# Two graph layers on one core: two row vectors are laid over the partitions through memory instead of by sixteen transposes, and the first unit of the score matrix is made later

## The chip, the cores and the metric

The kernel runs on one core of one Trainium2 chip. The metric is the device time of one execution in microseconds (us); lower is better.

## The reference, cut to what matters

Eight batches of a 1024 x 256 input `x` go through two graph layers. Layer 0 normalises `x`, builds a dense 1024 x 1024 matrix T from two score vectors and applies it twice. Layer 1 normalises again, adds the identity to the adjacency, scales it by row sums, and multiplies.

```python
def layer0(X, A):                       # X = relu(layernorm(x)), A = adj
    Xw = X @ Wv + bv
    sj, si = Xw @ aw[:d, 0], Xw @ aw[d:, 0]
    e = leaky_relu(sj[:, None, :] + si[:, :, None] + ab[0], 0.2)
    T = A * exp(e); T = T / (T.sum(-1, keepdims=True) + 1e-12)
    H, Xk = 0, X
    for k in range(3):
        H = H + Xk @ Wk[k] + bk[k]
        Xk = einsum('bij,bjd->bid', T, Xk)
    return relu(H)

def layer1(X, A):                       # X = relu(layernorm(x)) of the new x
    Ah = A + eye
    dh = rsqrt(Ah.sum(-1))
    return relu(einsum('bnm,bmf,fc->bnc', dh[:, :, None] * Ah * dh[:, None, :], X, kernel) + bias)
# x = x + layer0(...);  x = x + layer1(...)
```

## The kernel before, in words

Every product keeps single-precision accuracy by splitting both factors in a high and a low part and adding three products (high-high, high-low, low-high). So each tile that TensorE (PE) reads is rounded by ScalarE (ACT, "high") and its rest is taken by VectorE (DVE) or GpSimd (POOL, "low").

A batch b goes through four stages on PE, each written out by hand on each engine, with semaphores between them:

- **U** (`accumulate`, phase 0): eight chunks i of 24 matmuls, T times (X W2). Chunks 1 to 4 are each followed by one `out_product` of batch b-1 (six matmuls). After chunk 4 stands `rows_of_mean(b + 1)` (L1003): eight transposes that each turn one column of means `mv0[:, t, 0]`, broadcast to 128 columns, so that the 1024 means of batch b+1 lie as a row on all 128 partitions, in two banks of PSUM.
- **Dense** (`layer0_dense(b + 1)`, L1063): for eight tiles t six matmuls of 512 columns into `da` and six of 258 into `db`. Between the two of tile t, PE waits on `p0_ready` until DVE has read `db` of tile t-1 (there is one `db` bank), and then makes one transpose `si_rows(t - 1)` (L1015) of a column of scores. The last one, `layer0_end`, stands after the first chunk of V.
- **V** (`accumulate`, phase 1): eight chunks of 24 matmuls, T times the result of U.
- **Z** (`layer1_piece`): sixteen pieces of six matmuls of 512 columns. Piece q needs the rounded half tile `a_ready` and, for q under 8, the tile `hs_ready` of the normalised input.

The work for the next batch lies beside these stages. T of batch b+1 is made in eight units u: ACT adds the scores and applies the leaky function (`leaky`, four instructions on L471) and the exponential (`exponent`, L477), DVE multiplies with the adjacency (`t_prod`, L747), ACT rounds (`t_high`, L485) and DVE takes the rest (`t_low`, L752). The tables `SCORE_V`, `HIGH_V`, `PROD_V`, `LOW_V` say after which chunk of V each unit's step stands; unit 0 is scored inside the dense stage (after tiles 4 and 5) and multiplied there (after tile 6).

Layer norm of batch b+1 needs on DVE: `stats0_of` (L646, two tiles after each of chunks 0 to 3 of U, table `STATS_U`), `moments0` (L637, L641), and `centre` (L686), which takes the row of means off the transposed input `xt`, for its first two groups after chunks 5 and 6 of U. ACT rounds it (`centred_hi`, L403, ahead of chunks 6 and 7), DVE takes the rest (`centred_lo`, L692). The dense stage starts when group 0 of these is ready.

In U, ACT also sums the rows of the adjacency (`rows`, L502), in the order of `ROWS_U`: tile 2 after chunk 2, tiles 5 and 6 after chunk 4, tile 7 after chunk 5. SyncE (SP) issues the loads in one written order: in U it loads row tiles 4 to 7, each when the slot of tile t-4 is free, and after each stores one output tile of batch b-1. `g1_hi` (L524) is ACT's rounding of each chunk of U, `u_chunk` (L765 to L772) DVE's reading of it.

Of the kernel before, what the change touches and what calls it, by code (L numbers as in the profile page):

```python
# [5 lines left out]
F32 = mybir.dt.float32  # L6
# [13 lines left out]
def gnn_two_layers(nc, x, x_t, adj, adj_t, adj_z, wv_t, vecs, wk, bk, w_l1, bias_l1, out):  # L20
# [11 lines left out]
    SCORE_V = {-1: 1, 2: 2, 3: 3, 5: 4}  # L32
    HIGH_V = {1: (0, 1), 5: (2,)}
    PROD_V = {0: 1, 3: 2, 5: 3, 7: 4}
# [11 lines left out]
    STATS_U = {0: (0, 1), 1: (2, 3), 2: (4, 5), 3: (6, 7)}  # L46
# [14 lines left out]
    with ctx:  # L61
# [70 lines left out]
        bv_r = sb("bv_r", [P, KD, P])  # L132
        v_s = sb("v_s", [P, KD + 1, 2])
# [19 lines left out]
        mean_rows = [tp[:, r].rearrange("p k c -> p (k c)") for r in range(2)]  # L153
# [12 lines left out]
        def si_tile(t):  # L166
            return acc[:, SI_SLOT, t % 4 * P:(t % 4 + 1) * P]

# [35 lines left out]
        nb1_ready = sem("nb1_ready")  # L204
        xt_loaded = [sem(f"xt_loaded{g}") for g in range(NG)]
        x_loaded = [sem(f"x_loaded{g}") for g in range(NG)]
        mean_full, xt_centred = sem("mean_full"), sem("xt_centred")
# [40 lines left out]
        def _(sp):  # L248
# [99 lines left out]
        def _(pool):  # L348
# [26 lines left out]
            def batch(b, last):  # L375
                for i in range(NT):
                    g1_split(b, i)
                    if i == (3 if b > 0 else -1) and not last:
# [17 lines left out]
        def _(act):  # L396
            def centred_hi(g, b):
# [48 lines left out]
            def si_copy(b, g):  # L446
                act.wait_ge(si_full, b * NG + g + 1)
                nc.scalar.copy(si[:, g * 2 * P:(g + 1) * 2 * P],
                               acc[:, SI_SLOT, g % 2 * 2 * P:(g % 2 + 1) * 2 * P]).then_inc(si_ready, 1)

            def leaky(b, u):
# [13 lines left out]
                if u % 2 == 0:  # L465

                    act.wait_ge(si_ready, b * NG + u // 2 + 1)
# [22 lines left out]
            def layer0_dense(b, after):  # L490
                for t in range(NT):
# [3 lines left out]
                    if t % 2 == 0 and t > 0:  # L495
                        si_copy(b, t // 2 - 1)
# [19 lines left out]
            def batch(b, par, last):  # L516
                for i in range(NT):
                    if i == 0 and b > 0:
                        zt_high(b - 1, 1)
                    if i >= NT - 2 and not last:  # L520
# [12 lines left out]
                def after(t):  # L533
# [86 lines left out]
        def _(dve):  # L620
# [201 lines left out]
            def batch(b, par, left):  # L822
                last = left == 0
                for i in range(NT):
# [4 lines left out]
                    u_chunk(b, i)  # L829
                    if i in (NT - 3, NT - 2) and not last:  # L830
# [8 lines left out]
                    if not last and b > 0:  # L839
                        for t in STATS_U.get(i, ()):  # L840
                            stats0_of(b + 1, t)
                        if i == 3:
                            moments0(b + 1)
                def after(t):
# [135 lines left out]
        def _(pe):  # L980
# [22 lines left out]
            def rows_of_mean(b):  # L1003
# [5 lines left out]
                for t in range(NT):  # L1009
                    ins = nc.tensor.transpose(mean_rows[t // HJ][:, t % HJ * P:(t % HJ + 1) * P],  # L1010
                                              mv0[:, t, 0:1].to_broadcast([P, P]), ident[:, :])
                    if t % HJ == HJ - 1:
                        ins.then_inc(mean_full, 1)

            def si_rows(b, t):  # L1015

                if t == 0 and b > 0:

                    pe.wait_ge(g1_tmp_ready, b * NT)
                if t % 2 == 0 and t > 0:  # L1020

                    pe.wait_ge(si_ready, b * NG + t // 2)
                ins = nc.tensor.transpose(si_tile(t), sij[:, t, 1:2].to_broadcast([P, P]), ident[:, :])  # L1023
                if t % 2:
                    ins.then_inc(si_full, 1)
# [37 lines left out]
            def layer0_dense(b):  # L1063
# [3 lines left out]
                for g in range(NG):  # L1067
# [3 lines left out]
                    for s in range(2):  # L1071
# [13 lines left out]
            def layer0_end(b):  # L1085
                pe.wait_ge(p0_ready, b * NT + NT)
                si_rows(b, NT - 1)
# [30 lines left out]
            def accumulate(b, phase, i, read, before, ready, n, rhs):  # L1118
# [8 lines left out]
                for jt in range(NT):  # L1127
                    if ready is not None and i == 0:
# [8 lines left out]
            def batch(b, last):  # L1137

                pe.wait_ge(g2_ready, b * NT + NT)
                for i in range(NT):  # L1140
                    if i % 2 == 0:
# [3 lines left out]
                               lambda jt: (g2_hi[:, jt, :], g2_lo[:, jt, :]))  # L1145
                    if i in OUT_U and b > 0:
                        out_product(b - 1, OUT_U[i])
                    if i == HJ and not last:
                        rows_of_mean(b + 1)
# [3 lines left out]
                for i in range(NT):  # L1153
                    if i == 1 and not last:
                        layer0_end(b + 1)
# [93 lines left out]
```

## Time and profile before

| what | value |
| --- | --- |
| median of 3 runs | 773.25 us (772.89 to 774.9) |
| the profiled execution, its own time | 775.14 us |
| its span in the trace | 772.9 us |
| mean granted TensorE clock | 0.998 of full speed |
| DVE, ACT, POOL busy | 79%, 70%, 24% of the span |

The profiled execution is 2.24 us longer than its span and 1.89 us above the median. Times in rows are microseconds from the start of the span. PE is the matmul engine, PEld its weight load; matmuls overlap, so the distance between two starts, not the length of one, is what a matmul takes of PE's time. SPq and ACTq are the DMA issues of SP and ACT.

### The profile page before, as it was taken

The numbers are of one execution on the slowest core, as the hardware profiler recorded it, in microseconds if no ns is written. First come the engines' busy times: TensorE is split into PE (matmuls) and PEld (weight loads), VectorE is DVE, ScalarE is ACT, GpSimd is POOL, SyncE is SP. The second block draws the span as 40 slices with busy tenths as digits, with TensorE's granted clock in tenths as the row PEclk, the third lists the DMA queues.
The fourth block names the chain that finished last, engine by engine and source line by source line (L and its number), as shares of the span: only waits on it lengthen the run. The fifth ranks groups of instructions, "written<-read, shape, count | busy, mean of one in ns | idle before, by whom it ended". The sixth has DMA issues, their size and how long they took to land.

```text
span 772.9 us, 14177 instructions
## 1 busy us (share of the span) xinstructions
PE 758.8 (98%) x5190; PEld 695.6 (90%) x5190; DVE 610.9 (79%) x1420; ACT 539.6 (70%) x1051; POOL 183.9 (24%) x184
## 2 busy tenths in 40 slices
PE   8699999999999999999999999999999999999997
PEld 8498988989899898998989989899998989889986
DVE  6986888778896789967888678886888777895665
ACT  3988797567966679657785578856698567976351
POOL 1031240312403123130321405123050321402330
PEclk9999999999999999999999999999999999999999
DMA  6846339624497055970569505784148733356411
GB/s 226 298 137 193 120 132 320 225 96 137 138 317 263 20 154 177 299 243 1 177 208 302 187 13 184 255 272 150 69 144 303 240 118 109 133 209 210 140 62 54
DMA packets 60660, 135.93 MB, mean 176 GB/s; under 512 B 6320, under 2 KB 32304, under 8 KB 60592
## 3 DMA queue, kind: packets, MB, share of 16 engines
q1 hardware_dynamic: 51824, 104.35, 41.1%
q10 hardware_dynamic: 8768, 30.68, 11.4%
q8 instruction: 41, 0.67, 0.4%
q14 instruction: 27, 0.22, 0.1%
HBM read 126.62 MB, written 8.39 MB: 175 GB/s over the span
## 4 chain that ended last, share of the span: by engine, by line
PE 90%; DVE 4%; ACT 4%; issue 1%; DMA 1%; SPq 0%; DVEq 0%
PE acc L1132 16%; PE acc L1134 16%; PE acc L1133 16%; PE da L992 11%; PE db L992 6%; PE da L1102 4%; PE da L1100 4%; PE da L1101 4%; PE tp L1100 4%; PE tp L1102 4%; PE tp L1101 4%; ACT tg_e L471 2%; PE acc L1023 1%; ACT g_hi L439 1%; PE tp L1010 1%
## 5 line engine op out<-in xcount | busy, mean ns | idle before, releaser
L1132 PE MATMUL acc<-g_hi,t_hi 128*128 128x256 f32 (+1 forms) x1024 | 291.9, 285 | 2.8 <-DVE g_lo L721 2.8
L1134 PE MATMUL acc<-g_hi,t_lo 128*128 128x256 f32 (+1 forms) x1024 | 290.3, 284 | 0.0
L1133 PE MATMUL acc<-g_lo,t_hi 128*128 128x256 f32 x1024 | 289.6, 283 | 0.0
L1132 PEld LDWEIGHTS acc<-g_hi,t_hi 128*128 128x128 f32 x1024 | 194.1, 190 | 3.5 <-issue 3.2
L1133 PEld LDWEIGHTS acc<-g_lo,t_hi 128*128 128x128 f32 x1024 | 194.6, 190 | 0.3
L1134 PEld LDWEIGHTS acc<-g_hi,t_lo 128*128 128x128 f32 x1024 | 194.5, 190 | 0.0
L366 POOL TENSOR_TENSOR g_lo<-tmp,g_hi 128x256 fp32r<-128x256 f32 x64 | 58.6, 916 | 265.8 <-ACT g_hi L524 265.8
L471 ACT ACTIVATE tg_e<-si,sij 128x256 f32<-128x256 f32 x256 | 109.3, 501 | 4.0 <-DVE sij L708 4.0
L758 DVE TENSOR_TENSOR a_lo<-a_raw,a_hi 128x512 fp32r<-128x512 f32 x128 | 89.7, 720 | 25.1 <-ACT a_hi L514 25.1
L361 POOL TENSOR_TENSOR rstd<-ve,mhalf 128x2 f32<-128x2 f32 (+2 forms) x41 | 51.3, 1251 | 193.6 <-DVE ve L658 144.9
L524 ACT CAST g_hi<-tmp 128x256 fp32r<-128x256 f32 x64 | 25.9, 404 | 101.1 <-DVE tmp L772 101.1
L514 ACT CAST a_hi<-a_raw 128x512 fp32r<-128x512 f32 x128 | 76.9, 619 | 18.5 <-DVE a_raw L797 11.6
L372 POOL TENSOR_TENSOR hs_lo<-tmp,hs_hi 128x256 fp32r<-128x256 f32 x64 | 60.2, 960 | 81.0 <-ACT hs_hi L416 81.0
L477 ACT ACTIVATE tg_e<-tg_e 128x1024 f32<-128x1024 f32 x64 | 67.9, 1061 | 1.2
L747 DVE TENSOR_TENSOR t_raw<-tg_a,tg_e 128x1024 f32<-128x1024 f32 x50 | 60.9, 1219 | 9.7 <-ACT tg_e L477 9.7
L502 ACT ACTIVATE a_raw<-a_raw 128x1024 f32<-128x1024 f32 x64 | 67.3, 1053 | 0.0
L752 DVE TENSOR_TENSOR t_lo<-t_raw,t_hi 128x1024 fp32r<-128x1024 f32 x50 | 62.0, 1240 | 0.0
L412 ACT ACTIVATE tmp<-p,nb,rstd 128x256 f32<-128x256 f32 x64 | 34.9, 593 | 38.1 <-DVE nb L662 37.9
L485 ACT CAST t_hi<-t_raw 128x1024 fp32r<-128x1024 f32 x50 | 52.2, 1043 | 0.4 <-DVE t_raw L747 0.4
L765 DVE TENSOR_SCALAR row_t<-acc 128x1 f32<-128x1 f32 x64 | 9.9, 155 | 52.7 <-PE acc L1134 52.7
L726 DVE SCALAR_TENSOR_TENSOR g_lo<-da,rstd,g_hi 128x256 fp32r<-128x256 f32 x56 | 27.1, 484 | 30.1 <-ACT g_hi L439 30.1
L1100 PE MATMUL tp<-a_hi,hs_hi 128*128 128x512 f32 x128 | 50.8, 397 | 0.0
(146 smaller groups left out, 1635.0 us busy)
## 6 DMA issues: line engine op xcount, KB each, us to landing
a_raw<-adj_dram SPq DMA_DIRECT2D x64, 512.0 KB, 4.6
a_raw<-adj_z_dram SPq DMA_DIRECT2D x64, 512.0 KB, 3.9
tg_a<-adj_t_dram ACTq DMA_DIRECT2D x58, 512.0 KB, 4.4
x_o<-x_dram SPq DMA_DIRECT2D x64, 128.0 KB, 2.5
out_dram<-x_o SPq DMA_DIRECT2D x64, 128.0 KB, 3.5
x_nat<-x_dram SPq DMA_DIRECT2D x28, 256.0 KB, 4.3
xt<-x_t_dram SPq DMA_DIRECT2D x28, 256.0 KB, 4.5
tg_a<-adj_t_dram SPq DMA_DIRECT2D x6, 512.0 KB, 4.0
```

The costliest lines, as they stand in the source:

```text
L471: ins = nc.scalar.activation(tg_e[:, s, :, q, :], si[:, c].rearrange("p (s i) -> p s i", s=2), ACT.Prelu, bias=sij[:, jt, 0:1], alpha=SLOPE)
L477: nc.scalar.activation(tg_e[:, u % TS], tg_e[:, u % TS], ACT.Exp).then_inc(e_ready, 1)
L502: nc.scalar.activation(a_raw[:, t % RS, :], a_raw[:, t % RS, :], ACT.Copy, accum_out=row_a[:, t:t + 1]).then_inc(rows_done, 1)
L514: nc.scalar.copy(a_half(a_hi, i, h), a_raw[:, i % RS, h * N // 2:(h + 1) * N // 2]).then_inc(a_hi_done[h], 1)
L752: nc.vector.tensor_tensor(t_view(t_lo, u), t_parts(b, u), t_view(t_hi, u).bitcast(F32), ALU.subtract).then_inc(t_ready, 1)
L758: nc.vector.tensor_tensor(a_half(a_lo, i, h), a_raw[:, i % RS, h * N // 2:(h + 1) * N // 2], a_half(a_hi, i, h).bitcast(F32), ALU.subtract ...
L992: ins = nc.tensor.matmul(dst[:, 0:n], l, r, start=(c == 0 and a == 0), stop=(c == len(pairs) - 1 and a == 2))
L1100: nc.tensor.matmul(zt[r][:, f, :], l_hi, r_hi, start=(jt == 0), stop=False)
L1101: nc.tensor.matmul(zt[r][:, f, :], l_hi, r_lo, start=False, stop=False)
L1132: nc.tensor.matmul(acc[:, s, 0:n], l_hi, r_hi, start=(jt == 0), stop=False)
L1133: nc.tensor.matmul(acc[:, s, 0:D], l_hi, r_lo, start=False, stop=False)
L1134: ins = nc.tensor.matmul(acc[:, s, 0:n], l_lo, r_hi, start=False, stop=(jt == NT - 1))
```

## The change

The means of batch b+1 are turned with one transpose of `mv0[:, :, 0]` (128 x 8) into an 8 x 128 corner of PSUM. ACT copies it into SBUF (`mean_t`), SP stores it to a 4 KB tensor in memory (`mean_rows_dram`), waits until it has landed, and reads it back with one DMA that writes all 1024 means on each of the 128 partitions, into the buffer `si`, whose scores of batch b are no longer needed. `centre` takes the means from there. The transpose stands in the middle of chunk 3 of U (chunk 1 for the first batch). The statistics move to chunks 0 and 1 of U (four tiles each), and `rstd0` on POOL to chunk 1.

The scores go the same way in two halves of four tiles: one transpose ahead of `db` of tile 4 of the dense stage and one in the middle of chunk 0 of V, a copy of 4 x 128 by ACT, a store of 2 KB, and a read of 512 scores to all partitions.

The first unit of T is scored and multiplied after tile 7 of the dense stage; unit 1 moves in V from before chunk 0 to after it (scores) and from chunk 0 to 1 (product), its rounding from chunk 1 to 2.

```diff
-    SCORE_V = {-1: 1, 2: 2, 3: 3, 5: 4}
-    HIGH_V = {1: (0, 1), 5: (2,)}
-    PROD_V = {0: 1, 3: 2, 5: 3, 7: 4}
+    SCORE_V = {0: 1, 2: 2, 3: 3, 5: 4}
+    HIGH_V = {1: (0,), 2: (1,), 5: (2,)}
+    PROD_V = {1: 1, 3: 2, 5: 3, 7: 4}
-    STATS_U = {0: (0, 1), 1: (2, 3), 2: (4, 5), 3: (6, 7)}
+    STATS_U = {0: (0, 1, 2, 3), 1: (4, 5, 6, 7)}
 # SP
+            def mean_over_partitions(b):
+                sp.wait_ge(mean_t_ready, b)
+                sp.dma_start(mean_dram, mean_t).then_inc(mean_stored, 16)
+                sp.wait_ge(mean_stored, 16 * b)
+                sp.wait_ge(leaky_done, b * NU)
+                sp.dma_start(si[:, :], mean_dram.rearrange("t (o p) -> o (t p)", o=1).to_broadcast([P, N])).then_inc(mean_loaded, 16)
+            def si_over_partitions(b, h):
+                sp.wait_ge(si_t_ready, 2 * (b - 1) + h + 1)
+                sp.dma_start(si_dram[h], si_t).then_inc(si_stored, 16)
+                sp.wait_ge(si_stored, 16 * (2 * (b - 1) + h + 1))
+                sp.wait_ge(xt_centred, (b - 1) * NG + 2 * h + 2)
+                sp.dma_start(si[:, h * HJ * P:(h + 1) * HJ * P],
+                             si_dram[h].rearrange("(o t) p -> o (t p)", o=1).to_broadcast([P, HJ * P])).then_inc(si_loaded[h], 16)
             def batch(b, left):
                 for i in range(HJ):
                     rows(b, (RS + i,))
                     if b > 0:
                         stores(b - 1, HJ + i)
+                    if i == 1 and left > 0 and b > 0:
+                        mean_over_partitions(b + 1)
...
                 for i in range(NT):
+                    if i == 2 and left > 0:
+                        si_over_partitions(b + 1, 0)
+                        si_over_partitions(b + 1, 1)
 # ACT
+            def mean_copy(b):
+                act.wait_ge(mean_full, b)
+                nc.scalar.copy(mean_t, mean_bank).then_inc(mean_t_ready, 1)
+            def si_copy(b, h):
+                act.wait_ge(si_t_full, 2 * (b - 1) + h + 1)
+                if h == 1:
+                    act.wait_ge(si_stored, 16 * (2 * b - 1))
+                nc.scalar.copy(si_t, si_bank).then_inc(si_t_ready, 1)
                 for i in range(NT):
+                    if i == (1 if b == 0 else 3) and not last:
+                        mean_copy(b + 1)
...
-                    if t == 4 and not last:
-                        leaky(b + 1, 0)
-                    if t == 5 and not last:
-                        exponent(b + 1, 0)
                     if t == 7:
                         a_round(b, 1, 1)
+                        if not last:
+                            leaky(b + 1, 0)
+                            exponent(b + 1, 0)
 # DVE
-                dve.wait_ge(mean_full, 2 * (b - 1) + g // 2 + 1)
-                row = mean_rows[g // 2][:, g % 2 * 2 * P:(g % 2 + 1) * 2 * P]
+                dve.wait_ge(mean_loaded, 16 * b)
+                row = si[:, g * 2 * P:(g + 1) * 2 * P]
-                    if t == 6 and not last:
-                        t_prod(b + 1, 0)
                     if t == 7:
                         a_low(b, 1, 0)
                         a_low(b, 1, 1)
+                        if not last:
+                            t_prod(b + 1, 0)
 # PE
-                for t in range(NT):
-                    ins = nc.tensor.transpose(mean_rows[t // HJ][:, t % HJ * P:(t % HJ + 1) * P],
-                                              mv0[:, t, 0:1].to_broadcast([P, P]), ident[:, :])
+                nc.tensor.transpose(mean_bank, mv0[:, :, 0], ident[:, :]).then_inc(mean_full, 1)
+            def si_turned(b, h):
+                if h == 0:
+                    pe.wait_ge(g1_tmp_ready, b * NT)
+                else:
+                    pe.wait_ge(si_t_ready, 2 * b - 1)
+                pe.wait_ge(p0_ready, b * NT + HJ * (h + 1))
+                nc.tensor.transpose(si_bank, sij[:, h * HJ:(h + 1) * HJ, 1], ident[:, :]).then_inc(si_t_full, 1)
                         pe.wait_ge(p0_ready, b * NT + t)
-                        if t > 0:
-                            si_rows(b, t - 1)
+                        if t == HJ:
+                            si_turned(b, 0)
```

## Rows read from the trace of the kernel before

**Rows 1.** The page: busy time of PE, and the chain that ended last, by engine.

```profile
PE 758.8 (98%) x5190; PEld 695.6 (90%) x5190; DVE 610.9 (79%) x1420; ACT 539.6 (70%) x1051; POOL 183.9 (24%) x184
...
PE 90%; DVE 4%; ACT 4%; issue 1%; DMA 1%; SPq 0%; DVEq 0%
```

**Rows 2.** Groups by line of PE, shapes apart: busy us, mean ns.

```profile
L1023 PE MATMUL acc<-ident,sij 128*128 128x128 f32 x56 | 16.3, 292 | 0.7
...
L1010 PE MATMUL tp<-ident,mv 128*128 128x128 f32 x56 | 7.2, 272 | 0.0
```

**Rows 3.** The chain in order of time: start us, us of the span, what.

```profile
148.84 0.87 PE tp L1010 x8
...
158.32 1.39 PE da L992 x6
159.71 0.72 PE db L992 x6
```

**Rows 4.** The timeline of PE: first matmuls of U, dense, V and Z of batch 1.

```profile
131.44 0.28 PE L1132 MATMUL acc<-g_hi,t_hi 128*128 128x258 f32 x1
...
158.16 0.39 PE L992 MATMUL da<-wa_hi,ht_hi 128*128 128x512 f32 x1
...
176.40 0.28 PE L1132 MATMUL acc<-g_hi,t_hi 128*128 128x256 f32 x1
...
199.51 0.39 PE L1100 MATMUL da<-a_hi,hs_hi 128*128 128x512 f32 x1
```

**Rows 5.** Who waited for whom: us in total, times, longest.

```profile
PEld acc L1023 <- DVE sij L708: 10.1, 29, 0.5
```

**Rows 6.** The timeline of ACT and DVE in the dense stage: [idle before <- releaser].

```profile
169.51 0.37 ACT L448 COPY si<-acc 128x256 f32<-128x256 f32 x1
169.76 1.72 ACT L471 ACTIVATE tg_e<-si,sij 128x256 f32<-128x256 f32 x4
...
172.08 1.07 ACT L477 ACTIVATE tg_e<-tg_e 128x1024 f32<-128x1024 f32 x1
...
172.24 0.48 DVE L726 SCALAR_TENSOR_TENSOR g_lo<-da,rstd,g_hi 128x256 fp32r<-128x256 f32 x1 [0.58 <-ACT g_hi L439]
```

**Rows 7.** The timeline of ACT and DVE in U of batch 1.

```profile
136.77 0.74 DVE L646 BATCH_NORM_STATS2 st<-x_nat 128x6 f32<-128x256 f32 x2
...
142.45 1.06 ACT L502 ACTIVATE a_raw<-a_raw 128x1024 f32<-128x1024 f32 x1
...
147.11 0.65 DVE L637 BATCH_NORM_AGGREGATE mv<-st 128x2 f32<-128x6 f32 x8
...
153.84 1.06 ACT L502 ACTIVATE a_raw<-a_raw 128x1024 f32<-128x1024 f32 x1
...
154.89 0.61 ACT L403 ACTIVATE ht_hi<-xt 128x512 fp32r<-128x512 f32 x1
...
156.88 0.69 DVE L692 SCALAR_TENSOR_TENSOR ht_lo<-xt,ht_hi 128x512 fp32r<-128x512 f32 x1
```

**Rows 8.** DMA issues in windows at 146, 147, 151 and 162 to 181: KB, us to landing.

```profile
out_dram<-x_o SPq DMA_DIRECT2D x1, 128.0 KB, 2.1
...
a_raw<-adj_dram SPq DMA_DIRECT2D x1, 512.0 KB, 3.4
...
a_raw<-adj_z_dram SPq DMA_DIRECT2D x3, 512.0 KB, 4.8
...
x_o<-x_dram SPq DMA_DIRECT2D x1, 128.0 KB, 2.0
```

**Rows 9.** The timeline of ACT and DVE in V and at the start of Z.

```profile
177.68 1.71 ACT L471 ACTIVATE tg_e<-si,sij 128x256 f32<-128x256 f32 x4 [0.56 <-DVE sij L708]
...
191.36 1.22 DVE L747 TENSOR_TENSOR t_raw<-tg_a,tg_e 128x1024 f32<-128x1024 f32 x1 [1.05 <-ACT tg_e L477]
...
203.37 0.68 DVE L758 TENSOR_TENSOR a_lo<-a_raw,a_hi 128x512 fp32r<-128x512 f32 x1
...
206.49 2.44 DVE L758 TENSOR_TENSOR a_lo<-a_raw,a_hi 128x512 fp32r<-128x512 f32 x3 [0.55 <-ACT a_hi L514]
```

More of the change, by code:

```diff
@@ L132, in gnn_two_layers @@
         bv_r = sb("bv_r", [P, KD, P])
+        mean_t, si_t = bv_r[0:NT, 0, :], bv_r[0:HJ, 1, :]
         v_s = sb("v_s", [P, KD + 1, 2])
@@ L152, in gnn_two_layers @@
         zt = [da, tp.rearrange("p g k c -> p g (k c)")]
-        mean_rows = [tp[:, r].rearrange("p k c -> p (k c)") for r in range(2)]
+        mean_bank = tp[0:NT, 0, 0, 0:P]
+        si_dram = nc.dram_tensor("si_rows_dram", (2, HJ, P), F32, kind="Internal").ap()
+        mean_dram = nc.dram_tensor("mean_rows_dram", (NT, P), F32, kind="Internal").ap()
         ht_first = [g1.rearrange("p t d -> p (t d)").rearrange("p (g k c) -> p g k c", g=NG, k=KD) for g1 in (g1_hi, g1_lo)]
@@ L204, in gnn_two_layers @@
         nb1_ready = sem("nb1_ready")
+        si_t_full, si_t_ready, si_stored = sem("si_t_full"), sem("si_t_ready"), sem("si_stored")
+        si_loaded = [sem(f"si_loaded{h}") for h in range(2)]
         xt_loaded = [sem(f"xt_loaded{g}") for g in range(NG)]
         x_loaded = [sem(f"x_loaded{g}") for g in range(NG)]
-        mean_full, xt_centred = sem("mean_full"), sem("xt_centred")
+        mean_full, mean_t_ready, mean_stored, mean_loaded, xt_centred = (
+            sem(n) for n in ("mean_full", "mean_t_ready", "mean_stored", "mean_loaded", "xt_centred"))
         hs_hi_done, hs_ready = sem("hs_hi_done"), sem("hs_ready")
@@ L336, in _ @@
                         load_xt(1, g)
+            mean_over_partitions(1)
             for b in range(0, B - 3, 2):
@@ L377, in batch @@
                     g1_split(b, i)
-                    if i == (3 if b > 0 else -1) and not last:
+                    if i == (1 if b > 0 else -1) and not last:
                         power(rstd0, ve0, ve0_ready, b + 1, rstd0_ready)
@@ L464, in leaky @@
                     act.wait_ge(p0_ready, b * NT + (u + 1) * HJ)
-                if u % 2 == 0:
-                    act.wait_ge(si_ready, b * NG + u // 2 + 1)
+                if b == 0 and u % 2 == 0:
+                    act.wait_ge(si_ready, u // 2 + 1)
+                elif b > 0 and u % HJ == 0:
+                    act.wait_ge(si_loaded[u // HJ], 16 * b)
                 c = slice(u // 2 * 2 * P, (u // 2 + 1) * 2 * P)
@@ L494, in layer0_dense @@
                     dense0(b, t)
-                    if t % 2 == 0 and t > 0:
-                        si_copy(b, t // 2 - 1)
+                    if t == HJ:
+                        si_copy(b, 0)
                     after(t)
@@ L829, in batch @@
                     u_chunk(b, i)
+                    if not last and b > 0:
+                        for t in STATS_U.get(i, ()):
+                            stats0_of(b + 1, t)
+                        if i == 1:
+                            moments0(b + 1)
                     if i in (NT - 3, NT - 2) and not last:
@@ L838, in batch @@
                         t_low(b, low[i])
[L839 to L843, printed above, removed]
                 def after(t):
@@ L1116, in out_product, with accumulate @@
                                                     for f in range(KD)]).then_inc(out_full, 1)
-            def accumulate(b, phase, i, read, before, ready, n, rhs):
+            def accumulate(b, phase, i, read, before, ready, n, rhs, middle=None):
                 s = acc_slot(phase, i)
@@ L1127, in accumulate @@
                 for jt in range(NT):
+                    if jt == HJ and middle is not None:
+                        middle()
                     if ready is not None and i == 0:
@@ L1144, in batch @@
                     accumulate(b, U_PHASE, i, g1_tmp_ready, v_tmp_done, None, D + 2,
-                               lambda jt: (g2_hi[:, jt, :], g2_lo[:, jt, :]))
+                               lambda jt: (g2_hi[:, jt, :], g2_lo[:, jt, :]),
+                               middle=(lambda: rows_of_mean(b + 1)) if i == (1 if b == 0 else 3) and not last else None)
                     if i in OUT_U and b > 0:
                         out_product(b - 1, OUT_U[i])
-                    if i == HJ and not last:
-                        rows_of_mean(b + 1)
                 if not last:
@@ L1153, in batch @@
                 for i in range(NT):
-                    if i == 1 and not last:
-                        layer0_end(b + 1)
                     if i == 2 and not last:
-                        pe.wait_ge(si_ready, (b + 2) * NG)
+                        pe.wait_ge(si_t_ready, 2 * (b + 1))
                     accumulate(b, V_PHASE, i, v_tmp_done, g1_tmp_ready, g1_ready, D,
-                               lambda jt: (g1_hi[:, jt, :], g1_lo[:, jt, :]))
+                               lambda jt: (g1_hi[:, jt, :], g1_lo[:, jt, :]),
+                               middle=(lambda: si_turned(b + 1, 1)) if i == 0 and not last else None)
                 dense = b + 1 if last else b + 2
```

22 lines of the change are left out of this document (3 added, 19 removed).

## The prediction, made before the changed kernel was run

> **What bounds it now.** I read the page first, then the chain in order of time, the waits of PE, and the timeline of batch 1 with its four stages. PE is busy 758.8 of 772.9 us and holds 90% of the chain that ended last [rows 1]; the reader is to see that almost every matmul taken away is time taken away. Outside the first 40 us and the last 2 us PE has no waits but one kind: before the score transposes it waits for DVE's `sij`, 29 times, 10.1 us in total on the weight-load side [rows 5]. Much of that 10.1 us is the previous matmul still streaming, so it isn't the price; the stage's length is. The starts of the stages of batch 1 give U 26.72 us, dense 18.24, V 23.11, Z from 199.51 on [rows 4]. A tile of the dense stage needs 1.39 + 0.72 = 2.11 us of issue [rows 3], eight of them 16.9, so the dense stage holds 18.24 - 16.9 = 1.35 us of transposes and stalls.
>
> **What PE loses.** There are seven transitions to a next batch.
>
> Means: eight transposes take 0.87 us in the chain [rows 3], 0.11 each, though each lasts 272 ns [rows 2]. One remains: 0.76 us saved per transition, all of it on PE's path. I take for the new form (8 columns in, 8 x 128 out) the same 0.11; bounds 0.05 to 0.27 (its full length), a hundredth or so of the sum. The Trainium skill, "TensorE: Matmul & The Clock Gate", Part 4 on the PE-mode transpose, gives about 275 ns for one in a kernel's context. Its length agrees with the 272 ns of the trace, but thirteen removed per transition at 275 ns would be 25 us, and the distances in the chain say 0.11 each; the distances decide.
>
> Scores: of the seven in the dense stage one remains, and the one after chunk 0 of V remains inside it. Without waits that is 6 x 0.11 = 0.66 us. But `p0_ready` stays: PE waits there for DVE with or without a transpose. I went through the tiles on ACT and DVE. Around tile 3 DVE runs without a pause (a diagonal, `centred_lo`, `centre`, then the tile), so `db` of tile 3 starts where the transpose started, 8.1 us into the stage, and the 0.22 saved before becomes a stall of about 0.35. Behind it the stage runs freely, because the second stall goes: now ACT puts 1.71 us of `leaky` and an exponential of 1.06 us among tiles 4 and 5, after which DVE waits 0.58 us for ACT's `g_hi` and PE for DVE [rows 6]. Both move behind tile 7, and ACT also loses three copies of 0.37 [rows 6] here and gains one. New length: 16.9 + 0.11 + 0.35 = 17.4, so 0.85 saved per transition. The least is nothing at all (DVE as the pace, below), the most 1.24 (no stall).
>
> **What the mean's way through memory costs.** The cover is the rest of U, and the queues behind it are what matters. DVE now does eight statistics (0.37 each, the pair 0.74 with its overlap) and the aggregates (0.65 and the add) before chunk 2 where it did four [rows 7]: chunk 2 is read 2.1 us later, at 143.9 by the clock of this batch instead of 142.0. PE needs it only for chunk 5, at 149. ACT's rounding of chunk 2 and row sum 2, now at 142.45 [rows 7], end at 145.4, and `mean_copy` follows, 0.25 to 0.37 by the copy in [rows 6]: 145.7. The transpose at 143.1 is ahead of it. SP then stores 4 KB: the quiet store in [rows 8] takes 2.1 us for 128 KB, so 147.8. The read of 512 KB on all partitions: 3.4 us for one row tile alone, 4.8 for three in a row [rows 8], so 151.3 to 152.6, where `centre` stands at 152.7. Nearly free.
>
> SP waits while it does this, and row tiles 6 and 7 are behind it. Tile 6 is issued at 148.2 (now 143.6) and lands at 148.2 + 4.8 = 153.0 at most; ACT reaches its sum at 150.6 and waits. From its landing R: row sum 6 (1.15 with its read-out), `g1_hi` 0.3, row sum 7 1.15, `centred_hi` 0.6, `centred_lo` 0.7 [rows 7], so R + 3.9 = 156.9. PE is ready for the dense stage at 158.16 - 0.76 = 157.4. Slack 0.5 us; I take no stall, and every us beyond it is a us of stall per transition. In the trace of before the same `centred_lo` ends at 157.6, 0.6 ahead of PE. The Trainium skill, "DMA: Bandwidth & Descriptors", Anatomy of one DMA, puts a DMA at 2.0 us plus its bytes at 436 GB/s; an estimate from that page is 2.0 for the store and 3.2 for each 512 KB, which would leave the chain some 1.5 us more room than the rows do. It also says that the wait is "surprisingly long" above all for a write to HBM, which is the store here.
>
> The scores' first half: transposed 10.2 us into the stage, copied by 11.5, stored and read back by 2.1 + 2.0 to 3.4 [rows 8], at 15.6 to 17.0; memory traffic is idle there. Its reader, `leaky(0)`, stands at 18.0. Free. The second half is needed only for unit 4. SP's load of the residual tile for chunk 2 of V is behind both, 2 us later than now and still ahead of DVE.
>
> **What the later unit 0 costs.** After tile 7 ACT has `leaky` and `exponent` of unit 0 (2.7 us) and then of unit 1 (2.7) where it had only unit 1 [rows 9]. DVE waits for the first (`t_prod(0)` at 3.4 us into V), so chunk 0 is read 1.7 us later, which PE doesn't see (it needs it for chunk 3). `t_prod(1)`, 1.2 us, stands at chunk 1 ahead of both `t_low`; chunk 3 of V is read about 0.9 us later, and the product of unit 2, which waits for ACT already [rows 9], some 1.0 later in V. From there DVE had no pause of note until the first `a_lo` of Z at 203.37 to 204.05 [rows 9]. PE needs that for piece 4, at 199.51 + 4 x 1.39 = 205.1: slack 1.0. The next, at 206.49 to 207.2 [rows 9], is needed for piece 6 at 207.9: slack 0.7. So 1.0 later costs about 0.3 us of stall per transition. Bounds: 0 (the shift soaked up) to 1.0 (shift of 1.7, as at chunk 0).
>
> **Sum.** 0.76 + 0.85 - 0.3 = 1.3 us per transition, seven of them 9.2 us. The profiled execution's span of 772.9 would be 763.7, its own 775.14 some 765.9. The median lies 1.89 below the latter: 773.25 - 9.2 = 764.0 us. About 0.3% (2.3 us) is what a measurement here can tell from no change.
>
> **Rivals.**
> 1. The dense stage keeps its length, because `p0_ready` and not the transposes is its pace: the change doesn't do there what it says. For: DVE has no pause around tile 3. Against: before tiles 4 to 7 DVE waits for ACT and ACT for PE. Left are 0.76 x 7 = 5.3, without the stall in Z since V is no nearer: 768.
> 2. SP's queue: row tile 6 late by 0.5 to 1.5 beyond the slack. For: the slack is only 0.5 us and the chain goes through three landings, which vary from 2.0 to 4.8. Against: each was taken near its upper row. Cost 1 us per transition: 771; at 0.5 it is 767.5.
> 3. The tail of V shifts by the whole 1.7 us, the stall in Z is 1.0: 0.6 left per transition, 769.
> 4. The other side: the same queue, but memory is slow to confirm the store or to serve 128 reads of one 4 KB row. It decides once row tile 6 lands more than 0.5 + 1.3 + 0.33 = 2.1 us later than worked out, after 155.1; 2.5 us later in each transition costs 0.4 x 7 over the kernel before: 776. No row shows a read of one row by all partitions alone.
> 5. Neither stall comes and the dense stage reaches 17.0: 0.76 + 1.24 = 2.0, so 759.5.
>
> **Chances.** Forecast with its small deviations (762 to 766.5) 0.5; rival 1 0.1; 2 0.16; 3 0.08; 4 0.06; 5 0.1. Faster by over 0.3% (below 770.9): the forecast, 1, 3, 5 and half of 2, 0.85; within 0.3% 0.09, mostly of 2; slower 0.06. The range takes in the good part of 5 and of 2: 760.5 to 769.5.
>
> **What would show it.** PE's instructions fall by 13 x 7 = 91. The dense stage should be 17.4 long with its one pause at tile 3; U 25.95; `ht_lo` before the dense stage without a PE wait; ACT idle about 2.5 us for a row tile (L502) around chunk 4 of U, with a DMA as its releaser; in Z a pause of PE of some 0.3 at piece 6, released by `a_lo` L758. I am wrong if the first PE wait of a transition is at the start of the dense stage, if the dense stage stays above 18, or if Z grows by more than 0.5 us.

## The result, and the profile after

The changed kernel takes 777.45 us (median of 6 runs, 775.59 to 779.72), the kernel before 773.11 (6 runs): ratio 1.0049, 95% interval 1.003 to 1.0068. The forecast was 764.0, between 760.5 and 769.5. It is slower, and its runs spread over 4 us. The profiled execution of the kernel before is 1.9 us above its median, so the spans below differ by 2.6 us where the medians differ by 4.3.

The page of the changed kernel, as in [rows 1]:

```profile
PE 754.7 (97%) x5099; PEld 682.4 (88%) x5099; DVE 611.7 (79%) x1420; ACT 534.3 (69%) x1044; POOL 185.3 (24%) x184
...
PE 45%; DVE 25%; ACT 17%; issue 7%; DMA 3%; POOL 3%; SPq 0%; ACTq 0%; DVEq 0%; POOLq 0%
```

PE lost its 91 instructions and 4 us of busy time, the span grew from 772.9 to 775.5. The chain tells more: PE held 90% of it, now 45%, and DVE and ACT have 42%. PE now waits for them in every batch.

Where, the stage lengths say. They are distances between first matmuls of stages in the timeline, as in [rows 4]; the table gives means over batches 1 to 6 (U, V, Z of batch b, dense of batch b+1).

| kernel | U | dense | V | Z | time, us |
| --- | --- | --- | --- | --- | --- |
| before | 26.72 | 18.25 | 23.00 | 25.24 | 773.11 |
| forecast | 25.95 | 17.4 | 23.0 | 25.5 | 764.0 |
| changed | 26.82 (26.04 to 27.63) | 17.77 | 22.98 | 26.26 | 777.45 |

U is 26.04, 26.09, 26.11 in three transitions, near the forecast, and 27.47, 27.60, 27.63 in the other three. Z is 1.0 longer in all. The dense stage is 0.48 shorter, 0.37 less than forecast. The long Z and the long U take back everything that PE had gained.

**Ahead of the dense stage.** The timeline of PE, ACT and DVE of the changed kernel, batch 1:

```profile
156.25 0.28 PE L1167 MATMUL acc<-g_hi,t_lo 128*128 128x258 f32 x1
158.04 0.47 PE L1033 MATMUL da<-wa_hi,ht_hi 128*128 128x512 f32 x1 [1.50 <-DVE ht_lo L733]
...
152.69 1.06 ACT L542 ACTIVATE a_raw<-a_raw 128x1024 f32<-128x1024 f32 x1 [3.08 <-DMA a_raw<-adj_dram]
...
155.50 1.06 ACT L542 ACTIVATE a_raw<-a_raw 128x1024 f32<-128x1024 f32 x1 [1.36 <-DMA a_raw<-adj_dram]
...
156.56 0.61 ACT L438 ACTIVATE ht_hi<-xt 128x512 fp32r<-128x512 f32 x1
...
157.20 0.69 DVE L733 SCALAR_TENSOR_TENSOR ht_lo<-xt,ht_hi 128x512 fp32r<-128x512 f32 x1 [1.70 <-ACT ht_hi L438]
```

PE is through with U at 156.4 and stands until 158.04, because `ht_lo`, which DVE starts at 157.20, ends at 157.89. That waited for ACT's rounding at 156.56, which stands in ACT's order behind the sum of row tile 7 at 155.50, and that waited for its load. The issues of SP in the same stretch:

```profile
145.30 0.29 SPq L300 DMA_DIRECT2D mean_rows_dram<-bv_r  x1
146.54 0.33 SPq L304 DMA_DIRECT2D si<-mean_rows_dram  x1
146.92 0.44 SPq L268 DMA_DIRECT2D a_raw<-adj_dram  x1
147.40 0.43 SPq L273 DMA_DIRECT2D out_dram<-x_o  x1
147.88 0.44 SPq L268 DMA_DIRECT2D a_raw<-adj_dram  x1
```

and the landings, from narrow windows at 146.5 (the read of the means), 146.9 (row tile 6) and 147.9 (row tile 7):

```profile
si<-mean_rows_dram SPq DMA_DIRECT2D x1, 512.0 KB, 4.8
...
a_raw<-adj_dram SPq DMA_DIRECT2D x1, 512.0 KB, 5.8
...
a_raw<-adj_dram SPq DMA_DIRECT2D x1, 512.0 KB, 7.6
```

Batch 1 of the changed kernel starts U 1.03 us earlier than that of the kernel before (131.44 in [rows 4]), because the batch ahead of it is shorter:

```profile
130.41 0.28 PE L1165 MATMUL acc<-g_hi,t_hi 128*128 128x258 f32 x1
```

The forecast's instants are by the clock of the kernel before. So both are counted here from the start of U, in us:

| step of batch 1 | forecast | measured |
| --- | --- | --- |
| store of the means issued | 14.3 | 14.9 |
| read of the means issued | 16.4 | 16.1 |
| row tile 6 issued | 16.8 | 16.5 |
| row tile 6 landed | 21.6 at most | 22.3 |
| row tile 7 there for its sum | 23.0 | 25.1 |
| `ht_lo` ends | 25.5 | 27.5 |
| PE ready for the dense stage | 26.0 | 26.0 |

The store began 0.6 late and was faster than taken (1.24 us from its issue to the next one, not 2.1), so row tile 6 was issued 0.3 early. But it took 5.8 us and not 4.8, and landed 0.7 behind the forecast's latest; that alone uses up the slack of 0.5. Row tile 7 took 7.6 us. The forecast names no landing for it; its sum has the row sum of tile 7 start 1.45 behind the landing of tile 6, which is 23.0, and ACT waited 1.36 us for the tile.

The other transitions split by this one load. Row tile 6 lands at 21.8 to 22.0 in all of them. Row tile 7 takes 6.1 to 6.4 us in the three with a short U, where ACT doesn't wait for it, and 7.6 to 7.9 us in the three with a long one. What decides between the two values no run shows.

**In Z.** The timeline of PE of batch 1, changed kernel: pieces 4 and 6, and the first output product.

```profile
204.15 0.39 PE L1133 MATMUL da<-a_hi,hs_lo 128*128 128x512 f32 x1
204.71 0.50 PE L1131 MATMUL da<-a_hi,hs_hi 128*128 128x512 f32 x1 [0.17 <-DVE a_lo L799]
...
207.38 0.40 PE L1133 MATMUL da<-a_hi,hs_lo 128*128 128x512 f32 x1
207.83 0.50 PE L1131 MATMUL da<-a_hi,hs_hi 128*128 128x512 f32 x1
...
216.10 0.40 PE L1133 MATMUL tp<-a_hi,hs_lo 128*128 128x512 f32 x1
216.49 0.39 PE L1033 MATMUL db<-wl_hi,zt_hi 128*128 128x256 f32 x1
```

Starts here are 0.23 apart; before these three they are 0.56, 0.45 and 0.39, so 0.33, 0.22 and 0.16 too long. Behind each pause the first matmul is itself followed 0.10 us late. Together 1.0. The first two pauses are for `a_lo`, the third for `zt_lo` (L845), DVE's part of the first output product. The backlog that makes them, on DVE, rows to be held against 191.36 and 203.37 in [rows 9]:

```profile
191.95 1.23 DVE L788 TENSOR_TENSOR t_raw<-tg_a,tg_e 128x1024 f32<-128x1024 f32 x1 [1.07 <-ACT tg_e L517]
...
203.97 0.68 DVE L799 TENSOR_TENSOR a_lo<-a_raw,a_hi 128x512 fp32r<-128x512 f32 x1
```

V starts at 175.80 instead of 176.40 and Z at 198.78 instead of 199.51. So the product of unit 2 is 16.15 into V (before 14.96), 1.2 later, and the first `a_lo` of Z ends 5.87 into it (before 4.54), 1.3 later, where piece 4 needs it at 5.60.

From there on everything that DVE makes in Z stands 1.33 later than before, counted from the start of Z, down to `zt_lo`. First the kernel before, with the product that reads it, then the changed kernel:

```profile
216.29 0.28 PE L992 MATMUL db<-wl_hi,zt_hi 128*128 128x256 f32 x1
...
214.56 1.28 DVE L804 TENSOR_TENSOR zt_lo<-da,zt_hi 128x512 fp32r<-128x512 f32 x2
```

```profile
215.16 1.28 DVE L845 TENSOR_TENSOR zt_lo<-da,zt_hi 128x512 fp32r<-128x512 f32 x2
```

`zt_lo` ended 16.33 into Z and the product began at 16.78, 0.45 later; now it ends at 17.66 and the product begins at 17.71, 0.05 later. So only 0.40 us of a shift are free there, less than at piece 4 (1.0) or piece 6 (0.7), and the prediction did not price this place. PE stands 0.93 late at that product, the shift less 0.40, and 0.1 for the last restart makes the 1.02 by which Z grew. The pauses ahead of it are instalments of the same 0.93.

### The profile page after: what moved, and what is told of

Its sections match the earlier page's. It is cut to its first block, busy times and chain, and to the rows that moved or that the text cites. A ratio compares the mean times of both kernels' runs of the same rounds, so it can differ in the third digit from the quotient of the medians.

```text
span 775.5 us, 14030 instructions
## 1 busy us (share of the span) xinstructions
PE 754.7 (97%) x5099; PEld 682.4 (88%) x5099; DVE 611.7 (79%) x1420; ACT 534.3 (69%) x1044; POOL 185.3 (24%) x184
## 4 chain that ended last, share of the span: by engine, by line
PE 45%; DVE 25%; ACT 17%; issue 7%; DMA 3%; POOL 3%; SPq 0%; ACTq 0%; DVEq 0%; POOLq 0%
PE da L1033 10%; PE acc L1165 6%; PE acc L1167 6%; PE acc L1166 6%; PE db L1033 5%; ACT tg_e L511 5%; ACT tg_e L517 3%; DVE t_lo L793 3%; DMA a_raw<-adj_dram 3%; ACT tmp L447 3%; DVE t_raw L788 3%; PE tp L1131 2%; PE tp L1133 2%; PE tp L1132 2%; POOL hs_lo L402 2%
## 5 line engine op out<-in xcount | busy, mean ns | idle before, releaser
L542 ACT ACTIVATE a_raw<-a_raw 128x1024 f32<-128x1024 f32 x64 | 67.5, 1055 | 21.8 <-DMA a_raw<-adj_dram 21.6
L473 ACT ACTIVATE p<-da,rstd 128x256 f32<-128x256 f32 x56 | 26.6, 475 | 48.4 <-PE da L1033 48.2
L1131 PE MATMUL da<-a_hi,hs_hi 128*128 128x512 f32 x128 | 52.0, 407 | 1.6 <-DVE a_lo L799 1.0
```

The source lines that it names most:

```text
L1131: nc.tensor.matmul(zt[r][:, f, :], l_hi, r_hi, start=(jt == 0), stop=False)
```

## The experiments

Stage lengths of all of them, made as above, ahead of their single accounts:

| kernel | U | dense | V | Z | time, us | ratio to before (interval) |
| --- | --- | --- | --- | --- | --- | --- |
| a1 mean only | 26.80 (26.36 to 27.44) | 18.35 | 22.96 | 25.23 | 775.07 | 1.0011 (1.0001 to 1.0022) |
| a2 scores, unit 0 | 26.72 | 17.69 | 23.05 | 26.22 | 778.12 | 1.0055 (1.004 to 1.007) |
| a3 unit 0 only | 26.72 | 17.96 | 23.00 | 26.20 | 778.99 | 1.0067 (1.0052 to 1.0082) |
| a4 row tile 6 first | 26.96 (26.11 to 28.1) | 18.04 | 23.01 | 26.25 | 780.62 | 1.0087 (1.0072 to 1.0102) |
| b1 low 2 in Z | 26.38 (25.96 to 27.65) | 17.75 | 22.97 | 26.57 | 778.15 | 1.0055 (1.0035 to 1.0075) |
| b2 row sums later | 25.97 | 17.70 | 23.03 | 26.20 | 772.67 | 0.9978 (0.9968 to 0.9988) |
| b3 both | 25.97 | 17.71 | 23.00 | 26.46 | 774.38 | 1.0003 (0.9994 to 1.0012) |
| b4 mean, row sums later | 25.97 | 18.26 | 23.03 | 25.24 | 769.79 | 0.9944 (0.9929 to 0.9959) |
| c1 leaky ahead | 25.96 | 17.68 | 23.57 | 25.24 | 771.33 | 0.9957 (0.9944 to 0.997) |
| c2 distinct rows | 25.96 | 17.70 | 22.99 | 26.23 | 772.96 | 0.9988 (0.9975 to 1.0) |
| c3 ACT's queue | 25.97 | 17.68 | 22.96 | 26.27 | 772.58 | 0.9979 (0.997 to 0.9988) |
| d1 transpose later | 25.97 | 17.68 | 23.02 | 26.29 | 773.68 | 0.9994 (0.9985 to 1.0003) |

### a1, a2, a3: the change in parts

a1 puts on the kernel before the statistics, `rows_of_mean`, `mean_copy` and `mean_over_partitions` of the change, with one wait more, so that the old score copies don't overwrite means still to be read:

```diff
                 act.wait_ge(si_full, b * NG + g + 1)
+                act.wait_ge(xt_centred, (b - 1) * NG + g + 1)
```

> The kernel before with the means alone laid out through memory (statistics early, one transpose, SP's store and read back); scores and unit 0 as before. Theory 1 (two separate costs: the later unit 0 makes the pauses in Z, SP's round trip makes the pause ahead of the dense stage): Z stays at 25.24, dense at 18.2, U is 26.05 where row tile 7 lands in time and up to 27.6 where not; 768.5 to 773 us. Theory 2 (the 512 KB read of one 4 KB row slows all memory traffic and with it the whole next stages): Z or V grow here too, and the time is above 773.

a2 is the complement: `si_turned`, `si_over_partitions`, the new `si_copy` and the order of units 0 and 1, means as before. a3 takes of that the order alone:

```diff
-    SCORE_V = {-1: 1, 2: 2, 3: 3, 5: 4}
+    SCORE_V = {0: 1, 2: 2, 3: 3, 5: 4}
...
-                    if t == 4 and not last:
-                        leaky(b + 1, 0)
-                    if t == 5 and not last:
-                        exponent(b + 1, 0)
...
                         a_round(b, 1, 1)
+                        if not last:
+                            leaky(b + 1, 0)
+                            exponent(b + 1, 0)
```

> The kernel before with the scores through memory and the later unit 0; means by eight transposes as before. Theory 1: U stays 26.72 with no pause ahead of the dense stage, dense falls to 17.8, V by 0.1, Z grows to 26.25; net +0.4 per transition, 775.5 to 776.5 us. Theory 2: Z stays near 25.3 and the time falls to about 770.

> The kernel before with nothing but the order of units 0 and 1 changed (scores by transposes as before). Theory 1: Z grows to 26.2, dense loses its second stall (18.25 to about 17.95); net +0.7 per transition, about 778 us. Rival: Z's pauses come from the residual tiles or chunk loads that SP issues later behind its waits for the scores; then Z stays 25.24 and the time is 771 to 773.

The stages fall apart cleanly. The long Z belongs to a2 and a3 and not to a1; in a3 no score goes through memory, no SP issue has moved, and Z is 26.20. So the later unit 0 alone makes the pauses in Z, and the way of the scores through memory doesn't. The uneven U belongs to a1 alone. a1 came out 2 us above the range given for it, but not as theory 2 has it: Z and V did not grow, and its U is above 26.3 in all six batches of its profile. a2 and a3 were 1 to 2 us above theirs, with stages within 0.15 of those expected. Of each of these misses 0.9 us is the kernel before, which took 774.1 us beside these runs. a3 against a2 also prices the scores' way: without their transposes the dense stage is 0.27 shorter (17.96 to 17.69).

### a4: row tile 6 ahead of the mean, a miss

```diff
                     rows(b, (RS + i,))
+                    if i == 2 and left > 0 and b > 0:
+                        mean_over_partitions(b + 1)
                     if b > 0:
                         stores(b - 1, HJ + i)
-                    if i == 1 and left > 0 and b > 0:
-                        mean_over_partitions(b + 1)
```

> The changed kernel with row tile 6 issued ahead of SP's wait for the mean (the store and read back follow it). If the place in SP's order is what delays ACT: ACT no longer waits for row tile 6, the dense stage starts without a pause, U is 26.0 in every transition, 771 to 772 us. If the slow read itself is the cause (row tile 7 still behind it lands after 7 us): U stays between 26.1 and 27.5 and the time between 773 and 777.

Neither case: ACT no longer waits for row tile 6, but it is the slowest kernel of all. SP's issues of a4, batch 1:

```profile
145.88 0.33 SPq L268 DMA_DIRECT2D a_raw<-adj_dram  x1
146.25 0.33 SPq L300 DMA_DIRECT2D mean_rows_dram<-bv_r  x1
149.30 0.34 SPq L304 DMA_DIRECT2D si<-mean_rows_dram  x1
```

The same 4 KB store that took 1.24 us when the last load was issued 3.2 us ahead of it takes 3.05 us when a 512 KB load is issued 0.37 us ahead of it (2.9 to 3.3 in all six transitions). Counted from the start of U, the read of the means goes 2.0 us later and row tile 7 1.5 us later, and now `centre` waits for the means too:

```profile
153.74 0.69 DVE L727 TENSOR_TENSOR xt<-xt,si 128x512 f32<-128x512 f32 x1 [1.30 <-DMA si<-mean_rows_dram]
...
155.35 1.06 ACT L542 ACTIVATE a_raw<-a_raw 128x1024 f32<-128x1024 f32 x1 [2.47 <-DMA a_raw<-adj_dram]
```

ACT waits for tile 7 alone, and that is enough: U is 26.10 to 28.10. One dense stage of this profile, from 628.04 on, was 19.33 long. There PE's granted clock was 0.50, its lower level of 1.2 GHz, after PE had stood idle for 1.98 us, the longest pause ahead of a dense stage in this profile (columns: length, PE, PEld, DVE, ACT, POOL busy, clock, DMA share, GB/s):

```profile
629.00:631.50 2.50, 2.50 (x11) 2.21 (x10) 1.09 (x3) 1.20 (x4) 1.27 (x1) 0.50 0.46 166
```

The stage lost 1.5 us by it in this execution.

### b2, b4: ACT's order

```diff
-    ROWS_U = {0: (0,), 1: (1,), 2: (2,), 3: (3, 4), 4: (5, 6), 5: (7,)}
+    ROWS_U = {0: (0,), 1: (1,), 2: (2,), 3: (3, 4), 4: (5,), 5: (6,), 6: (7,)}
```

b2 is this line on the changed kernel, b4 on a1.

> The changed kernel with ScalarE's sums of row tiles 6 and 7 one chunk later, so that row tile 7 is no longer ahead of the rounding of the centred input. SP's order and all DMAs stay. If the path is row tile 7's landing, ScalarE's order, start of the dense stage: U is 25.9 to 26.1 in every transition, Z stays 26.25; about 773.5 to 774.5 us with little spread between runs. If instead the read of the means itself lands too late: U keeps its values of up to 27.6.

> The kernel with the means alone through memory, and ScalarE's sums of row tiles 6 and 7 one chunk later. Two separate costs: U 26.0, dense 18.3, V 23.0, Z 25.24, about 0.7 us per transition less than before: 769 us.

No DMA moved, and U is 25.97 in every batch of both. The sum of row tile 7 now stands behind the first rounding of the centred input, and its landing no longer reaches PE. b2's ten runs lie between 772.52 and 772.87; the 4 us of spread are gone with the wait. b4 keeps the old unit 0, has the short U and the short Z, and at 769.79 is the fastest kernel of the study. b2 came out 0.8 us below its range, b4 0.8 above its figure.

### c2, c3: what made row tile 7 late

c2 keeps every issue and wait, but reads 128 different rows of 4 KB in place of the same one 128 times (what is subtracted as the mean in the first layer norm of batches 1 to 7 is then not the mean, so its output is not that of the reference):

```diff
-                sp.dma_start(si[:, :], mean_dram.rearrange("t (o p) -> o (t p)", o=1).to_broadcast([P, N])).then_inc(mean_loaded, 16)
+                sp.dma_start(si[:, :], adj_v[b, :, 0]).then_inc(mean_loaded, 16)
```

> The changed kernel, but the read of the means takes 512 KB from 128 different rows of the adjacency in place of 128 times the same 4 KB row (so the first layer norm subtracts other numbers than the means). All waits, issues and bytes stay. If the repeated row is slow to read: this transfer lands in about 3.5 instead of 4.8 us, row tiles 6 and 7 land 1 us earlier, U is 26.0 in nearly all transitions, 773.5 to 774.5 us. If only the place in the queue counts: landings and time as in the changed kernel, 775.5 to 779.

The transfer lands in 4.2 us (median of seven) instead of 4.6, row tile 6 behind it in batch 1 in 5.0 instead of 5.8, row tile 7 in 5.6 to 5.9 in all six transitions instead of 6.1 to 7.9, and U is 25.96 or 25.97 throughout its profile. The stretch from 149 to 151, first of the changed kernel, then of c2 (PE, PEld, DVE, ACT, POOL busy, clock, DMA share, GB/s):

```profile
149.00:151.00 2.00, 2.00 (x19) 2.00 (x19) 0.16 (x1) 0.62 (x2) 0.58 (x1) 1.00 0.94 244
```

```profile
149.00:151.00 2.00, 2.00 (x19) 2.00 (x18) 0.36 (x1) 1.00 (x2) 0.93 (x1) 1.00 0.91 330
```

With nearly the same share of the DMA engines' time, the kernel with the repeated row moves 244 GB/s and the other 330. At the same place of batch 2 (243.1 to 245.1, and 241.8 to 243.8 in c2) it is 211 GB/s at a share of 0.75 against 337 at 1.00. So a part of row tile 7's delay is the repeated row: in batch 1 it lands in 5.9 us and not 7.6, which is most of what it took beyond 4.8, and ACT waits 0.35 us for it and not 1.36. One of c2's ten runs took 776.22; it was not the profiled one, so whether the wait came back in it is not shown.

c3 has ACT issue the store (chunk 3 of U) and the read (chunk 4) of the means from its own queue:

```diff
                 nc.scalar.copy(mean_t, mean_bank).then_inc(mean_t_ready, 1)
+                act.wait_ge(mean_t_ready, b)
+                act.dma_start(mean_dram, mean_t).then_inc(mean_stored, 16)
```

> The changed kernel with the store of the means and their read issued by ScalarE (the store at chunk 3 of U, the read at chunk 4) instead of SP, so that SP waits for neither. If SP's waits delay the row tiles: row tile 6 is issued 2 us earlier and ScalarE doesn't wait for it, row tile 7 lands by 153, U is 26.0 to 26.1, about 773 us. If the transfers themselves crowd the row tiles out: ScalarE still waits for row tile 7 and U stays up to 27.5.

U is 25.97, and ACT waits for no row tile in batches 1 to 6. The read goes 1.5 us later from the start of U (at 148.44), now behind row tile 7, and takes 5.4 us, so DVE waits for it instead, which PE doesn't notice:

```profile
153.78 0.69 DVE L734 TENSOR_TENSOR xt<-xt,si 128x512 f32<-128x512 f32 x1 [1.68 <-DMA si<-mean_rows_dram]
```

So SP's round trip ahead of the two loads, the repeated row and ACT's order are three conditions of one stall, and taking away any one of them is enough (for the repeated row, in nine of ten runs). Moving the round trip behind row tile 6 alone, as in a4, is not enough.

### b1, b3, c1, d1: the pauses in Z

b1 takes DVE's `t_low` of unit 2 out of V; b3 is b1 with the later row sums.

```diff
-    LOW_V = {1: 0, 2: 1, 6: 2}
+    LOW_V = {1: 0, 2: 1}
-    LOW_Z, LOW_U = {1: 3, 7: 4, 12: 5, 15: 6}, {1: 7}
+    LOW_Z, LOW_U = {1: 2, 3: 3, 7: 4, 12: 5, 15: 6}, {1: 7}
```

> The changed kernel with the low part of unit 2 taken after piece 1 of Z instead of after chunk 6 of V (and that of unit 3 after piece 3), 1.2 us less for VectorE ahead of the first tiles that Z waits for. If VectorE's backlog from the later unit 0 makes the pauses in Z: Z falls from 26.25 to about 25.3, U and dense as in the changed kernel; 777.4 - 6.5 = 771 us. If the pauses have another source (the residual tiles or chunks of the adjacency landing late): Z stays at 26.25.

> Both edits on the changed kernel. Theory of two separate costs: U 26.0, dense 17.8, V 23.0, Z 25.3, that is 1.25 us per transition less than the kernel before: 765 us. If the two costs hide one another, or a third wait stands behind them: above 768 us.

Wrong as a cure. The pause at piece 4 goes, a longer one stands at piece 6, and Z is 0.3 longer than without the edit. (b1 also kept the stall of U, 27.65 in one batch.) b3, batch 1, PE, ACT and DVE:

```profile
207.10 0.50 PE L1131 MATMUL da<-a_hi,hs_hi 128*128 128x512 f32 x1 [0.65 <-DVE a_lo L799]
...
204.10 0.60 ACT L447 ACTIVATE tmp<-p,nb,rstd 128x256 f32<-128x256 f32 x1 [1.55 <-DVE nb L703]
...
203.91 0.16 DVE L703 SCALAR_TENSOR_TENSOR nb<-mv,rstd 128x2 f32<-128x2 f32 x1 [0.59 <-POOL rstd L391]
...
206.35 1.84 DVE L799 TENSOR_TENSOR a_lo<-a_raw,a_hi 128x512 fp32r<-128x512 f32 x2 [0.54 <-ACT a_hi L554]
...
200.26 0.16 DVE L699 SCALAR_TENSOR_TENSOR ve<-mv,row_a 128x2 f32<-128x2 f32 x1
...
200.33 2.43 POOL L402 TENSOR_TENSOR hs_lo<-tmp,hs_hi 128x256 fp32r<-128x256 f32 x2 [1.91 <-ACT hs_hi L451]
202.73 1.14 POOL L391 TENSOR_TENSOR rstd<-ve,mhalf 128x2 f32<-128x2 f32 x1
```

DVE has time now, and waits itself: for ACT's `a_hi`, ACT for `nb`, `nb` for POOL's `rstd`. The input of `rstd`, `ve`, is there at 200.42, but POOL first works off two `hs_lo`, and takes 2.43 us for them (1.60 in the changed kernel). Why these took longer was not tested. Everything behind is then 1.55 late instead of 1.33: taking 1.2 us from one engine only names the next.

That a shift, and not the number of pauses, sets Z can be read from `zt_lo` of batch 1 in five kernels:

| kernel | `zt_lo` ends, us into Z | later than before | less 0.40, plus 0.10 | Z longer than before |
| --- | --- | --- | --- | --- |
| before | 16.33 | | | |
| c1 (below) | 16.50 | 0.17 | none | 0.00 |
| changed | 17.66 | 1.33 | 1.03 | 1.02 |
| d1 (below) | 17.79 | 1.46 | 1.16 | 1.17 |
| b3 | 17.88 | 1.55 | 1.25 | 1.24 |

c1 gets the backlog out where it comes in. With the later row sums of b2, unit 0's leaky function stands ahead of tile 7 of the dense stage (the scores have landed at 174.0 in the changed kernel, 170.86 + 3.1), and unit 1's product and rounding are back in chunks 0 and 1:

```diff
-    HIGH_V = {1: (0,), 2: (1,), 5: (2,)}
-    PROD_V = {1: 1, 3: 2, 5: 3, 7: 4}
+    HIGH_V = {1: (0, 1), 5: (2,)}
+    PROD_V = {0: 1, 3: 2, 5: 3, 7: 4}
...
+                        if not last:
+                            leaky(b + 1, 0)
                     if t == 7:
                         a_round(b, 1, 1)
                         if not last:
-                            leaky(b + 1, 0)
                             exponent(b + 1, 0)
```

> The changed kernel with ScalarE's sums of row tiles 6 and 7 one chunk later (as in b2), and unit 0 earlier: its leaky function ahead of tile 7 of the dense stage (its scores have landed by then), its exponential behind it, and product and rounding of unit 1 back in chunks 0 and 1 of V. Theory: the pauses in Z come from ScalarE's and VectorE's backlog of about 1.1 us that unit 0 brings into V, whichever chain it comes through. Then Z falls to 25.25 to 25.6 and the dense stage stays 17.7 to 17.9: 772.7 - 5 = 766 to 768 us. If Z stays above 26.1, the backlog is not the cause.

Z is 25.24, as before the change, and the dense stage stays at 17.68: the backlog theory holds. The time is 3.3 us above the range, for a new wait in V, which is 0.57 longer in batches 1 to 6 and 1.5 longer than b2's in the first. c1, batch 1:

```profile
177.25 0.27 PE L1061 MATMUL acc<-ident,sij 128*4 128x128 f32 x1 [0.50 <-DVE sij L750]
```

The second score transpose, in the middle of chunk 0 of V, waits for tile 7's scores, which are later now that ACT does the leaky function first. d1 puts it behind the chunk:

```diff
-                               middle=(lambda: si_turned(b + 1, 1)) if i == 0 and not last else None)
...
+                    if i == 1 and not last:
+                        si_turned(b + 1, 1)
```

> The kernel of c1 with the second score transpose behind chunk 0 of V instead of in its middle. In c1 TensorE stood 0.7 us there in each V (23.57 against 22.97), waiting for VectorE's last tile of the dense stage. If that wait is only a matter of place: V falls to 23.0, U, dense and Z stay at 25.97, 17.7 and 25.25; 771.3 - 4 = 767.3 us. If ScalarE, which now waits for this transpose ahead of unit 1, brings the backlog back: Z grows to 25.5 or more and the time stays above 769.

The second case: V is short, Z long again. ACT's copy of these scores stands ahead of unit 1 and now waits for the transpose:

```profile
178.25 0.26 ACT L486 COPY bv_r<-acc 4x128 f32<-4x128 f32 x1 [0.77 <-PE acc L1061]
```

The copy is 0.7 us later on ACT, and V is 0.6 shorter on PE, so Z starts 0.6 earlier. The two together turn a Z without a pause into one with three. Not tried: the copy behind unit 1's exponential.

## Why the prediction was wrong

- **What bounds it, and PE's saving: right.** 91 instructions went. In its undisturbed form U is 25.96 to 25.97 (forecast 25.95), so a transpose costs 0.11, and the 8-column form no more.
- **The dense stage: right in direction and place, short in size.** 17.77 instead of 17.4, so 0.48 saved and not 0.85. The stall at tile 3 is there (0.29 us where 0.35 was taken), the one of ACT's leaky function is gone (a3 alone gives 0.3). Left out was about 0.1 us that PE loses behind a wait, four times in a stage. Rival 1 is refuted.
- **The mean's way, first failed step.** "Tile 6 is issued at 148.2 (now 143.6) and lands at 148.2 + 4.8 = 153.0 at most" and the "row sum 7 1.15" behind it, as if its load were there, were the mis-sized terms. The 4.8 is a median of three loads of the adjacency for Z, and the trace of before already had a longer landing in U, row tile 5 of batch 3:

```profile
a_raw<-adj_dram SPq DMA_DIRECT2D x1, 512.0 KB, 5.5
```

Behind the read of the means tile 6 took 5.8 us and tile 7 7.6 us in batch 1. Tile 6 used up the slack of 0.5 and cost 0.1 to 0.3 us; where tile 7 took 7.6 us or more, it cost some 1.5 more. This is rival 2, with tile 7 for most of it in the place of tile 6. U of batches 1 to 6 is 160.9 us in the changed kernel and 155.8 in b2, 5.1 us of stalls in the profiled execution; the spans are 775.5 and 770.3.

- **The later unit 0, second failed step and the larger one.** "So 1.0 later costs about 0.3 us of stall per transition" was the mis-sized term (the way of the shift from unit 0 through V into the first `a_lo` is as written). It cost 1.0 per transition, 7 us in all: the shift was 1.33 and not 1.0, which is 0.3 more; the tightest slack was the 0.4 at the first output product, which the prediction left out, and not the 0.7 at piece 6, again 0.3; and 0.1 goes to the last restart. Rival 3 had this price, but for a shift of 1.7 us. a3 shows the term by itself: Z +0.96, dense -0.29, times seven 4.7, measured 1.0067 x 773, 5.2 us.
- **The two together.** b4, which has neither cost and goes without the dense gain, wins 4.3 us (interval 3.2 to 5.5) where seven times 0.76 are 5.3; c1 has the dense gain and no cost in Z, and loses 6 x 0.57 + 1.5 = 4.9 us in V.
- **The chances.** I gave 0.06 to slower, for memory slow to store or to serve the repeated row. The store was fast; the repeated row was slow, but mattered as one condition of the stall, not as its price. Two of the three signs of being wrong appeared: the first PE wait of a transition is at the start of the dense stage, and Z grew by more than 0.5 us. What I lacked was the case in which two small slacks both run out, taken as 0.5 and 0.7 us.

## What to carry to other kernels

When PE is saturated, work taken off it moves every deadline forward, so each slack of the other engines has to be measured against the new starts. A shift that runs through a whole stage is paid once, as the shift less the smallest slack of all places where PE reads from the other engines, however many pauses it falls into; so the list of those places has to be complete. A wait put into the written order in which SP issues its transfers is priced by the last load behind it and by what that load's reader holds up in its own order; moving the reader (one line of a table here) took the ratio from 1.0049 to 0.9978. Split a change before judging it: the mean part and one reordered table gave 769.8 us, under both kernels, while the scores' part lost through a reordering that isn't a transfer at all.

## What the runs showed of the hardware

- A small store's time depends on what was issued ahead of it: 4 KB to memory took 1.24 us from its issue to SP's next one with the last load issued 3.2 us ahead, and 3.05 us issued 0.37 us behind a 512 KB load (a4). The Trainium skill, "DMA: Bandwidth & Descriptors", Anatomy of one DMA, gives a fixed cost of about 2.0 us whatever the size, for DMAs that GpSimd issues; these two, issued by SP, lie on both sides of it.
- Reading one 4 KB row to all 128 partitions was slower than reading 128 rows: 4.6 against 4.2 us to landing, and 244 against 330 GB/s in the same 2 us of batch 1.
- A load of 512 KB issued 1.3 to 1.5 us behind the read of the repeated row landed after 6.1 to 6.4 us or after 7.6 to 7.9 us, three times each in one execution of the changed kernel, and after 5.6 to 5.9 us behind the read of distinct rows.
- After a pause of PE of 0.2 to 0.3 us in Z, the first matmul of 512 columns lasted 0.50 instead of 0.40 us, and the next started 0.33 instead of 0.23 us behind it, so each such wait cost 0.1 us beyond itself.
- PE's granted clock fell to 0.50 in one dense stage of a4, after an idle pause of 1.98 us; behind the next longest, of 1.85 us in the same execution, it did not fall.
